# A two-layer vision tower on one core: order of small steps in three of its stages

## The chip, the cores and the metric

One Trainium2 chip, one of its cores. The metric is the device time of the program in microseconds (us), the median of several runs. The program is written out engine by engine: TensorE (PE), VectorE (DVE), ScalarE (ACT), GpSimd (POOL) and SyncE (SP) each have a queue of their own that runs in the order in which it is written, and the queues meet at semaphores.

## The reference

Four images of 3 x 224 x 224 become 4 x 3136 tokens of width 192. In short:

```python
h = conv_patches(x)                      # 4 x 4 patches, 192 wide
h = proj(softmax(q k^T / sqrt(96)) v)
n = layernorm(h)
q, k = elu(n Wq) + 1, elu(n Wk) + 1      # 64 wide, q times 1/8
F = clip(cumsum(log(sigmoid(n Wf + bf))), -20, 20)
num = q . (exp(F) cumsum(exp(-F) k v^T)) ;  den = q . (exp(F) cumsum(exp(-F) k)) + 1e-6
h = h + layernorm(num / den, gamma, beta) Wo
n = layernorm(h)
p = softmax(gelu(n w1 + b1) w2 + b2)     # 8 experts, the best two, renormalised
h = h + layernorm(n + sum_e p_e up_e(gelu(down_e(n))), gamma, beta)
n = layernorm(h)
q, k, v = split(n Wqkv)                  # q, k divided by their L1 sums over the tokens
h = h + (q (k^T v) per head) Wproj + b
n = layernorm(h)
h = h + bitlinear(silu(gate) * up)       # weights to -1, 0, 1; activations to 8 bits
```

All of it is computed in float32 or in pairs of rounded parts (a high part and a low part that is the rest), except for the rounded products of the last layer.

## The kernel before, in words

Tokens are handled in groups of 448 (four rows of 112 tokens), 7 to an image and 28 in all (`NC`). `h` stays in on-chip memory for all tokens. There are four stages, each with its own block of engine programs.

**Patch attention**, up to about 860 us. The change doesn't touch it.

**Routing stage** (`attend_route_phase`), a loop of 28 steps and a tail of three to four. In step g VectorE works on several groups at once: the decayed attention of group g and g+1, the addition of group g-1 into `h` (`add_out`, two halves), and the choice of experts for group g-3 (`largest`, `choose`, `take_rank`, `places`, `share`). `places` makes the row numbers at which a token's two copies go (`idx`), `share` (lines 1249 to 1254) the tickets: for each copy its gate and the number of its token. The queue of GpSimd has, in each step,

```python
if here(g - 4): scatter(g - 4, 0)   # waits for the ticket; copy, four indirect DMAs
if here(g - 1): factor(g - 1)       # waits for agg; veps, then rst (lines 712, 714)
if here(g):     add_bias(g)
if here(g - 4): scatter(g - 4, 1)
if here(g - 1): factor_route(g - 1)
```

`scatter` (lines 733, 737) copies the ticket behind the normalised rows and writes 448 rows to `rows_in` in DRAM. `factor` makes the scale `rst` of group g-1 from the aggregates `agg` (line 1147) that VectorE has made at the end of step g-1; `add_out` (line 1192) needs it. The first half of `add_out` releases the products into its PSUM bank on TensorE, whose chain (lines 842 to 847) ends in `den` (line 1127).

**Tile stage** (`tile_phase`): 63 tiles of 448 routed rows, each through one expert. SP loads the rows (`xb`) and the expert's weights (`wd`) two tiles ahead, TensorE transposes and multiplies, ScalarE makes high parts and gelu, VectorE the low parts (`take_low`, lines 1589 and 1590, and `lower`, line 1614), the copies of gate and home row (`take_tail`, lines 1599 to 1606) and half of the scaled result `yb` (`take_y`, line 1624). GpSimd gives the rows back to `rows_out` with four indirect DMAs a tile (line 1578). `take_tail(t+1)` waits until the give-back of tile t-3 has returned, since it overwrites the row numbers; `take_y(t-1)` waits for the same, since it overwrites `yb`. The load of tile t+2 waits for the tail of tile t.

**Last stage** (`attention_and_ffn_phase`), 28 steps and then the FFN. In a step, GpSimd starts two transfers that add the two expert rows of each token to what is in `sums` (`add_rows`), then one that adds beta to `h` (`add_bet`), all for five steps ahead; normalised rows are transposed, and `q_and_k` makes three products of which VectorE and ScalarE take L1 sums (`a_sum`, `b_sum`). Each image ends with its solution, five small links on TensorE (`turn_gram`, `keys_map`, `values_map`, `project_map`, `image_map`) that write to `pqk[1]`, the bank that also holds product m == 1 of `q_and_k`, so that each waits for `b_sum` in places. The Gram matrices have two banks `pg`. At the start GpSimd fills six constants, among them a row of ones of `xTB` (1 x 4480); VectorE sums and rounds the FFN's weights (`sum_weights`, from line 2425, and `round_weights`, up to line 2444) ahead of the loop.

Of the kernel before, what the change touches and what calls it, by code (L numbers as in the profile page):

```python
# [555 lines left out]
def attend_route_phase(nc, ins, h, bns, mean, rstd, minus, eye, held, tile_e, tile_r, down,  # L556
# [6 lines left out]
    with ExitStack() as ctx:  # L563
# [532 lines left out]
        def _(dve):  # L1096
# [218 lines left out]
            for g in range(NC + 3):  # L1315
# [19 lines left out]
                if here(g - 3):  # L1335
                    places(g - 3)
                    share(g - 3)
# [16 lines left out]
                if here(g):  # L1354
                    sums_stats(g, (2, 3))
                    sums_aggr(g)

# [18 lines left out]
def tile_phase(nc, ins, eye, down, tile_e, tile_r, rows_in, rows_out, held, returned):  # L1376

    with ExitStack() as ctx:
# [206 lines left out]
        def _(dve):  # L1585
# [65 lines left out]
def attention_and_ffn_phase(nc, ins, h, bns, mean, rstd, var, minus, eye, rows_out, out):  # L1651
# [9 lines left out]
    with ExitStack() as ctx:  # L1661
# [49 lines left out]
        pg = [ps(f"pg4_{i}", [128, 512]) for i in range(2)]  # L1711
# [45 lines left out]
        def pga(g, q):  # L1757
            return pqk[q % 2 if g else 0]

        pup = pg  # L1760
# [16 lines left out]
        NW = 5  # L1777
# [28 lines left out]
        def _(pool):  # L1806
            for n, (buf, value) in enumerate(((eps5[:], 1e-5), (mhalf[:], -0.5), (xTB[RB:RB + 1], 1.0),
                                              (wl[64:128, 1, :].bitcast(F32), 0.0))):
                nc.gpsimd.memset(buf, value).then_inc(S["w_ready"], 1)
                pool.wait_ge(S["w_ready"], n + 1)  # L1810
            nc.gpsimd.memset(ones[:], 1.0).then_inc(F["set"], 1)
            pool.wait_ge(F["set"], 1)
            nc.gpsimd.memset(mhalf5[:], -0.5).then_inc(F["set"], 1)
            pool.wait_ge(F["set"], 2)
# [34 lines left out]
            pool.wait_ge(S["e_in"], 32)  # L1849
            for s in range(-LEAD, NC):  # L1850
                if here(s + 5):
                    add_rows(s + 5, 0)
                if here(s + 3):
                    factor(s + 3)
                if here(s + 5):
                    add_bet(s + 5)
                    add_rows(s + 5, 1)
                if here(s + 2):
                    factor4(s + 2)

# [29 lines left out]
        def _(pe):  # L1890
            pe.wait_ge(S["w_in"], 16 * NW)
            pe.wait_ge(S["w_ready"], 4)
# [13 lines left out]
            def gram(g, b, c):  # L1906
# [3 lines left out]
                for q in range(TPC):  # L1910
                    for i in range(2):

                        mm = pe.matmul(pg[i][:, 0:(D, RB)[i]], xn[g % 2][:, q, i * 128:(i + 1) * 128],
# [841 lines left out]
```

## Time and profile before

| | |
|---|---|
| median of three runs | 2668.47 us (2668.48, 2668.47, 2664.71) |
| the profiled execution | 2666.92 us |
| its span, first to last instruction | 2665.1 us |
| mean granted clock of TensorE | 0.912 of full speed |
| busy: TensorE, VectorE, ScalarE, GpSimd | 2250.9, 1924.3, 1594.4, 1040.1 us |
| scatter transfers to `rows_in` (L737) | 224 instructions, 235.1 us on GpSimd |
| give-back transfers to `rows_out` (L1578) | 252 instructions, 244.5 us on GpSimd |

The profile has one row for a run of like instructions: start in us from the span's start, duration, engine, line, operation, names, and in brackets how long the engine was idle before it and what ended that idle time. A line number is one of the kernel before. Of an idle time the last releaser is named, and a name is that of the buffer that it wrote. A window row gives the busy time of each engine in a stretch, so engines that are all below the stretch's length are in a loop of waits.

### The profile page before, as it was taken

How to read it: one execution, taken by the hardware profiler on the slowest of the kernel's cores; microseconds unless marked ns; L12 is line 12 of the kernel's file. 1: busy time of each engine (PE TensorE's matmuls, PEld its weight loads, DVE VectorE, ACT ScalarE, POOL GpSimd, SP SyncE). 2: the span in 40 equal slices, each digit the busy share in tenths (PEclk: the TensorE clock that was granted, in tenths of full speed). 3: DMA queues.
4: the chain of work that ended last, by engine and by line, in shares of the span. 5: the costliest groups of instructions: out<-in, count | busy, mean ns of one | idle time of the engine just before them, and what ended most of it. 6: DMA issues, size and time to landing. Idle time of an engine off the chain costs nothing. (4 is left out here: it accounts for less than half of the span.)

```text
span 2665.1 us, 45416 instructions
## 1 busy us (share of the span) xinstructions
PE 2250.9 (84%) x14046; PEld 1626.4 (61%) x14047; DVE 1924.3 (72%) x5417; ACT 1594.4 (60%) x2815; POOL 1040.1 (39%) x1101
## 2 busy tenths in 40 slices
PE   8999999999997899999982999991778887766655
PEld 4444444444443788888871999991667775544443
DVE  5777777777774688888872566664558778889896
ACT  2444444444443688888861676663778764667776
POOL 1100100100000167667673577676555533353433
PEclk9999999999998899999985999996779998777777
DMA  2000000000000333233235677777756720000000
GB/s 59 0 19 13 0 18 13 1 9 1 0 0 23 87 66 75 67 73 76 66 71 165 219 242 240 246 242 133 94 71 87 91 30 6 22 22 26 22 27 26
DMA packets 114522, 183.08 MB, mean 69 GB/s; under 512 B 14337, under 2 KB 84326, under 8 KB 114078
## 3 DMA queue, kind: packets, MB, share of 16 engines
q0 software_dynamic: 74816, 86.34, 17.3%
q1 hardware_dynamic: 39554, 94.84, 11.1%
q8 instruction: 80, 1.31, 0.2%
q14 instruction: 72, 0.59, 0.1%
HBM read 64.44 MB, written 64.39 MB: 48 GB/s over the span
## 5 line engine op out<-in xcount | busy, mean ns | idle before, releaser
L213 ACT ACTIVATE prob<-pscore 128x896 f32<-128x896 f32 x336 | 308.1, 917 | 423.5 <-PE pscore L295 423.5
L420 DVE TENSOR_REDUCE pmax<-ppre 112x1 f32<-112x512 f32 x656 | 424.3, 686 | 162.0 <-PE ppre L262 161.9
L309 PE MATMUL pout<-prob,xkey 128*64 128x448 f32 x1344 | 328.0, 567 | 0.4 <-ACT prob L213 0.4
L1578 POOL DMA_INDIRECT rows_out<-yb,home3b x252 | 244.5, 970 | 141.8 <-issue 59.3
L262 PE MATMUL ppre<-xh,yh 49*112 49x512 f32 x656 | 291.3, 446 | 7.8 <-DVE pmax L420 4.1
L195 POOL CAST yh<-ynext 113x448 fp32r<-113x448 f32 x28 | 17.2, 616 | 667.3 <-DVE pmax L420 639.2
L737 POOL DMA_INDIRECT rows_in<-xr,idx x224 | 235.1, 1050 | 76.3 <-issue 44.8
L262 PEld LDWEIGHTS ppre<-xh,yh 49*112 49x112 f32 x656 | 112.6, 172 | 239.5 <-issue 103.5
L295 PE MATMUL pscore<-yh,xh 49*128 49x448 f32 x700 | 241.2, 422 | 0.4 <-DVE yh L440 0.4
L1872 POOL TENSOR_TENSOR sums<-rows,gout 112x512 f32<-112x512 f32 x112 | 141.2, 1270 | 253.2 <-DVE rows L2501 253.2
L295 PE MATMUL pscore<-yh,xl 49*128 49x448 f32 x700 | 202.9, 364 | 0.0
L295 PE MATMUL pscore<-yl,xh 49*128 49x448 f32 x700 | 142.8, 364 | 0.0
L2060 PE MATMUL ptr<-eyeb,wT 112*128 112x112 bf16 x448 | 45.3, 292 | 114.1 <-ACT wT L2253 114.1
L1485 PE MATMUL pz<-xth3b,wd 128*128 128x448 f32 x504 | 140.7, 381 | 0.0
L1500 PE MATMUL py<-uph,zl 128*112 x504 | 131.8, 261 | 0.0
L1500 PE MATMUL py<-upl,zh 128*112 x504 | 131.6, 261 | 0.0
L1500 PE MATMUL py<-uph,zh 128*112 x504 | 131.5, 261 | 0.0
L309 PEld LDWEIGHTS pout<-prob,xkey 128*64 128x64 f32 x1344 | 66.6, 135 | 105.7 <-issue 85.3
L295 PEld LDWEIGHTS pscore<-yh,xl 49*128 49x128 f32 x700 | 127.9, 187 | 0.8
L1935 PE MATMUL pqk<-xh,wh 128*128 128x448 f32 x168 | 72.1, 429 | 56.4 <-ACT spent L2196 55.8
L2060 PEld LDWEIGHTS ptr<-eyeb,wT 112*128 112x128 bf16 x448 | 38.9, 141 | 126.8 <-ACT wT L2253 88.9
L1472 PE MATMUL ptr3b<-eye,xb 112*128 112x112 f32 x504 | 63.5, 271 | 61.9 <-DMA xb<-rows_in 42.8
(393 smaller groups left out, 6647.2 us busy)
## 6 DMA issues: line engine op xcount, KB each, us to landing
wd<-down SPq DMA_DIRECT2D x63, 512.0 KB
xb<-rows_in SPq DMA_DIRECT2D x63, 455.0 KB
sums<-rows_out POOLq DMA_DIRECT2D x56, 336.0 KB, 6.1
h<-brow POOLq DMA_DIRECT2D x28, 336.0 KB, 5.2
h<-gambet POOLq DMA_DIRECT2D x28, 336.0 KB, 4.9
out<-sums SPq DMA_DIRECT2D x28, 336.0 KB, 2.8
rows_in<-zero SPq DMA_DIRECT2D x15, 455.0 KB, 5.5
rows_out<-yb,home3b POOLq DMA_INDIRECT x252
```

Of the source, the lines that this page charges most:

```text
L213: nc.scalar.activation(prob[j % 3][:, :, :], pscore[j % 2][:, :, 0:CH], ACT.Exp).then_inc(exped, 1)
L262: pe.matmul(out[:, :], yh1[rows, q * T:(q + 1) * T], xh[b % 2][rows, block * 512:(block + 1) * 512], start=True, stop=True, tile_position= ...
L295: mm = pe.matmul(pscore[j % 2][:, i, 0:CH], x[b % 2][rows, keys], y[rows], start=(n == 0), stop=(n == 2), tile_position=(i * LO, 0))
L309: mm = pe.matmul(pout[i * LO:(i + 1) * LO, 0:CH], xkey[b % 2][:, 2 * j + i, :], prob[j % 3][:, i, :], start=(j == 0), stop=(i == 1 and j = ...
L420: nc.vector.reduce_max(pmax[:, q, 2 * block + half:2 * block + half + 1], bank(u, depth), AX.X).then_inc(pre_max, 1)
L737: nc.gpsimd.indirect_dma_start(rows_in, bass.IndirectOffsetOnAxis(ap=idx[r % G3][:, 2 * q + k:2 * q + k + 1], axis=0), xr[r % G3][:, q, :] ...
L1485: mm = pe.matmul(pz[m][:, 0:CH], wd[i][:, w, cols], x, start=(s_ == 0), stop=(s_ == 4))
L1500: mm = pe.matmul(py[i][:, q // 2, (q % 2) * D:(q % 2 + 1) * D], zz[i][m][:, cols], w[:, bass.ds(2 * e + m, 1), :], start=(m + n == 0), sto ...
L1578: nc.gpsimd.indirect_dma_start(rows_out, bass.IndirectOffsetOnAxis(ap=home[r][:, q:q + 1], axis=0), yb[r % 2][:, q, :], None).then_inc(ret ...
L1872: nc.gpsimd.tensor_tensor(yg5[:, q, :], y[:, q, :], gout[:], ALU.mult).then_inc(F["yg_out"], 1)
L1935: mm = pe.matmul(pqk[m % 2][:, 0:CH], w, x, start=(n == 0), stop=(n == 4))
L2060: mm = pe.transpose(pyt[:, half, k * CH + q * T:k * CH + (q + 1) * T], yq[:, q, (2 * half + k) * 128:(2 * half + k + 1) * 128], eyeb[0:T, ...
```

## The change

Five things change. (1) In the routing stage VectorE's `share` goes, in the 28 full steps, from behind `places` to the very end of the step, behind the aggregates; `largest` waits for the earlier ticket to be done. GpSimd's queue there stays. (2) In the tile stage VectorE makes both sets of low parts first, then the copies of gate and home row. (3) In the last stage the two Gram banks become one and the solution gets a bank of its own, `psol`; waits of TensorE that kept the shared bank go. (4) The second accumulating transfer of a group is started one step after the first. (5) At that stage's start the row of ones comes by transfer, the constants are filled later, and the weight sums and rounding move to the ends of steps -1 and 0.

```diff
             def largest(r):
 
                 dve.wait_ge(R["ex_out"], r + 1)
+                if r:
+                    dve.wait_ge(R["tail_out"], r)
...
                 if here(g - 3):
                     places(g - 3)
-                    share(g - 3)
+                    if g >= NC:
+                        share(g - 3)
...
                 if here(g):
                     sums_stats(g, (2, 3))
                     sums_aggr(g)
+                    if here(g - 3):
+                        share(g - 3)
...
             def tile(t, r, n, last=False, enter=True):
                 i = r % 2
                 if not last:
-                    take_tail(t + 1, (r + 1) % 4, n + i)
                     take_low(t + 1, 1 - i)
                 lower(t, r)
+                if not last:
+                    take_tail(t + 1, (r + 1) % 4, n + i)
...
-        pg = [ps(f"pg4_{i}", [128, 512]) for i in range(2)]
+        pgram = ps("pg4", [128, 512])
+        pg = [pgram[:, 0:D], pgram[:, D:D + RB]]
+        psol = ps("psol4", [128, 512])
...
-        def pga(g, q):
-            return pqk[q % 2 if g else 0]
-
-        pup = pg
+        pga = pqk
+
+        def pup(g, q):
+            return (pgram, psol)[q % 2 if g else 0]
...
             for dst, name in ((wT, "wT4"), (wq, "wq4"), (wpT, "wpT4"), (heads[:], "heads"),
-                              (wimg[RB:RB + 1, 1, :], "bproj4")):
+                              (wimg[RB:RB + 1, 1, :], "bproj4"), (xTB[RB:RB + 1], "unit")):
                 sp.dma_start(dst, ins[name]).then_inc(S["w_in"], 16)
+            sp.wait_ge(both_in[0], 16)
...
-            pool.wait_ge(S["e_in"], 32)
             for s in range(-LEAD, NC):
                 if here(s + 5):
                     add_rows(s + 5, 0)
+                if here(s + 4):
+                    add_rows(s + 4, 1)
                 if here(s + 3):
                     factor(s + 3)
+                if s == -LEAD:
+                    pool.wait_ge(S["e_in"], 32)
                 if here(s + 5):
                     add_bet(s + 5)
-                    add_rows(s + 5, 1)
                 if here(s + 2):
                     factor4(s + 2)
+                if s == 1 - LEAD:
+                    constants(filled[2:3])
+                if s == -1:
+                    nc.gpsimd.memset(ones[:], 1.0).then_inc(F["set"], 1)
...
                     elif m == 1 and g:
                         pe.wait_ge(S["b_sum"], g)
-                        if b and c <= 2:
-                            pe.wait_ge(S[("t2_out", "m1_out", "wi_out")[c]], b)
...
             def turn_gram(b):
 
                 pe.wait_ge(S["g_out"], b + 1)
-                pe.wait_ge(S["b_sum"], CPI * (b + 1))
-                pe.transpose(pqk[1][:, 0:128], gsb[:, 0, D - 128:D], eye[:]).then_inc(S["gt_mm"], 1)
+                if b:
+                    pe.wait_ge(S["wi_out"], b)
+                pe.transpose(psol[:, 0:128], gsb[:, 0, D - 128:D], eye[:]).then_inc(S["gt_mm"], 1)
...
                 pe.wait_ge(S["t2_out"], b + 1)
-                if b + 1 < B:
-                    pe.wait_ge(S["b_sum"], CPI * (b + 1) + 1)
...
                 pe.wait_ge(S["m1_out"], b + 1)
-                if b + 1 < B:
-                    pe.wait_ge(S["b_sum"], CPI * (b + 1) + 2)
...
                 if 1 <= g * TPC + q <= TPC:
-                    pe.wait_ge(F["sg_out"], g * TPC + q)
+                    pe.wait_ge(F["y_out"], g * TPC + q)
...
-            weights_summed()
             for s in range(NC):
...
                 q_and_k(s, b, c)
+                if s == 0:
+                    weights_summed()
...
-            sum_weights()
-            round_weights()
             dve.wait_ge(S["e_in"], 32)
             for s in range(-3, NC):
...
+                if s == -1:
+                    sum_weights()
+                if s == 0:
+                    round_weights()
```

The order of VectorE's instructions at two places, and of GpSimd's at one. First VectorE in the middle of a full step of the routing stage, before (`idx` the row numbers, `ticket` the tickets, `gate` the forget gates' input):

```order
L1269 CAST idx_0<-row 112x8
L1249 SCALAR_TENSOR_TENSOR both<-total,both 112x4
L1252 TENSOR_SCALAR ticket_0<-home 112x8
L1253 RECIPROCAL both<-both 112x4
L1254 TENSOR_TENSOR ticket_0<-top,both 112x8
L1153 TENSOR_SCALAR gate<-pff,bff 128x448
```

And VectorE after the change, at the end of the step and the start of the next:

```order
L1147 BN_AGGR agg<-bn 112x2 x4
L1251 SCALAR_TENSOR_TENSOR both<-total,both 112x4
L1254 TENSOR_SCALAR ticket_0<-home 112x8
L1255 RECIPROCAL both<-both 112x4
L1256 TENSOR_TENSOR ticket_0<-top,both 112x8
L1183 TENSOR_TENSOR at<-pat,mask 112x448
L1234 TENSOR_REDUCE total<-ex 112x4
L1236 MAX top<-ex 112x8 x4
L1238 TENSOR_TENSOR both<-top 112x4
L1192 SCALAR_TENSOR_TENSOR h<-pvo,rst,h 112x192 x2
```

The four instructions of `share` have moved behind the aggregates; the half-add at line 1192 is the next step's.

VectorE in a tile of the tile stage, before:

```order
L1599 TENSOR_SCALAR other3b<-xb_1 112x4
L1601 COPY gate3b<-xb_1 112x4
L1604 TENSOR_TENSOR home3b<-xb_1,other3b 112x4
L1589 TENSOR_TENSOR xtl3b<-ptr3b,xth3b 128x448
L1590 TENSOR_TENSOR xth3b<-ptr3b,xth3b 64x448
L1614 TENSOR_TENSOR zl<-z_0,zh 128x448
L1614 TENSOR_TENSOR zl<-z_1,zh 128x448
L1624 TENSOR_SCALAR yb_1<-py_1,gate3b 112x192 x2
```

and after:

```order
L1594 TENSOR_TENSOR xtl3b<-ptr3b,xth3b 128x448
L1595 TENSOR_TENSOR xth3b<-ptr3b,xth3b 64x448
L1619 TENSOR_TENSOR zl<-z_0,zh 128x448
L1619 TENSOR_TENSOR zl<-z_1,zh 128x448
L1604 TENSOR_SCALAR other3b<-xb_1 112x4
L1606 COPY gate3b<-xb_1 112x4
L1609 TENSOR_TENSOR home3b<-xb_1,other3b 112x4
L1629 TENSOR_SCALAR yb_1<-py_1,gate3b 112x192 x2
```

The three instructions of the tail stand now directly ahead of `yb`.

GpSimd at the start of the last stage, after the change, with its waits (the six fills stood in a row ahead of the first transfer before):

```order
L1820 MEMSET eps_3 112x4
L1820 MEMSET mhalf 112x4 [waits w_ready_4]
L1833 DMA sums<-rows_out 112x4x192 [waits xa_out_4,w_ready_4]
L1838 DMA h<-gambet 112x4x192 [waits e_in_4]
L1833 DMA sums<-rows_out 112x4x192 [waits xa_out_4]
L1833 DMA sums<-rows_out 112x4x192 [waits rstd_out_3]
L1838 DMA h<-gambet 112x4x192
L1820 MEMSET wl 64x384
```

Four of the fills are behind the first transfers or gone, and the second transfer of the first group comes behind the first of the next.

## Rows read from the trace of the kernel before

**Rows 1.** Windows: start:end, length, busy (x instructions) of PE, PEld, DVE, ACT, POOL; PEclk, DMA share, GB/s

```profile
1150.00:1390.00 240.00, 227.03 (x1576) 202.04 (x1574) 203.77 (x872) 191.77 (x349) 168.82 (x202) 0.98 0.33 72
1472.60:1799.20 326.60, 313.93 (x2481) 297.23 (x2479) 204.55 (x501) 227.54 (x414) 228.12 (x235) 1.00 0.75 241
1823.00:1870.00 47.00, 4.09 (x18) 4.03 (x19) 23.56 (x71) 19.71 (x42) 31.88 (x32) 0.50 0.97 161
```

**Rows 2.** Timeline, VectorE, one step of the routing stage

```profile
1258.04 0.74 DVE L1192 SCALAR_TENSOR_TENSOR h<-pvo,rst,h 112x192 f32<-112x192 f32 x2 [0.24 <-POOL rst L714]
...
1264.81 0.23 DVE L1127 TENSOR_SCALAR den<-pvo 112x2 f32<-112x2 f32 x2 [0.39 <-PE pvo L847]
...
1267.26 0.15 DVE L1249 SCALAR_TENSOR_TENSOR both<-total,both 112x4 f32<-112x4 f32 x1
...
1267.82 0.68 DVE L1153 TENSOR_SCALAR gate<-pff,bff 128x448 f32<-128x448 f32 x1
...
1274.25 0.38 DVE L1147 BATCH_NORM_AGGREGATE agg<-bn 112x2 f32<-112x6 f32 x4
...
1276.14 0.74 DVE L1192 SCALAR_TENSOR_TENSOR h<-pvo,rst,h 112x192 f32<-112x192 f32 x2 [0.25 <-POOL rst L714]
```

**Rows 3.** Timeline, GpSimd, the same step

```profile
1275.06 1.05 POOL L714 TENSOR_TENSOR rst<-veps,mhalf 112x4 f32<-112x4 f32 x1
```

**Rows 4.** Timeline, TensorE, the same step

```profile
1257.96 1.47 PE L865 MATMUL pvo<-wo,nT 96*112 96x192 f32 x8
...
1264.28 0.49 PE L847 MATMUL pvo<-snap,qt 128*112 128x193 f32 x2
```

**Rows 5.** Timeline, VectorE, step 28 of the routing stage

```profile
1375.65 0.17 DVE L1254 TENSOR_TENSOR ticket<-top,both 112x8 f32<-112x8 f32 x1
...
1377.23 0.38 DVE L1147 BATCH_NORM_AGGREGATE agg<-bn 112x2 f32<-112x6 f32 x4
...
1382.76 0.74 DVE L1192 SCALAR_TENSOR_TENSOR h<-pvo,rst,h 112x192 f32<-112x192 f32 x2 [4.60 <-POOL rst L714]
```

**Rows 6.** Timeline, TensorE, two places of the last stage

```profile
1904.39 2.32 PE L1913 MATMUL pg<-xn 112*128 112x192 f32 x16
...
1925.97 0.74 PE L1935 MATMUL pqk<-xh,wh 128*128 128x448 f32 x1 [4.16 <-ACT spent L2196]
...
1929.49 3.34 PE L1913 MATMUL pg<-xn 112*128 112x192 f32 x16
```

**Rows 7.** Windows around those places

```profile
1926.00:1929.40 3.40, 3.40 (x13) 3.08 (x14) 0.79 (x2) 2.30 (x6) 2.27 (x2) 0.50 1.14 146
1932.90:1934.90 2.00, 2.00 (x10) 1.51 (x9) 1.50 (x7) 2.00 (x6) 0.93 (x2) 1.00 0.00 0
```

**Rows 8.** Waits, 1472.6 to 1799.2 us: total us, times, longest

```profile
DVE other3b L1599 <- DMA rows_out<-yb,home3b: 59.5, 29, 3.2
```

**Rows 9.** Timeline, VectorE, two tiles of the tile stage

```profile
1598.88 0.17 DVE L1599 TENSOR_SCALAR other3b<-xb 112x4 f32<-112x4 f32 x1 [2.07 <-DMA rows_out<-yb,home3b]
...
1600.48 1.38 DVE L1614 TENSOR_TENSOR zl<-z,zh 128x448 fp32r<-128x448 f32 x2
...
1609.93 0.23 DVE L1599 TENSOR_SCALAR other3b<-xb 112x4 f32<-112x4 f32 x1 [2.25 <-DMA rows_out<-yb,home3b]
```

**Rows 10.** Timeline, GpSimd, the first give-back between them

```profile
1602.91 0.93 POOL L1578 DMA_INDIRECT rows_out<-yb,home3b  x1 [1.00 <-DVE yb L1624]
```

**Rows 11.** Waits, TensorE, 1950 to 2200 us

```profile
PE pqk L1991 <- DVE sums L2583: 2.1, 3, 0.8
PE pqk L2009 <- DVE sums L2583: 1.8, 2, 0.9
```

**Rows 12.** Timeline, VectorE, start of the last stage

```profile
1834.20 0.06 DVE L2425 MEMSET wsum<- 128x4 f32 x1 [2.02 <-DMA xTA<-in_wout]
...
1844.07 0.56 DVE L2444 TENSOR_SCALAR woutq<-xTA 128x768 bf16<-128x768 f32 x1
```

**Rows 13.** Timeline, GpSimd, start of the last stage

```profile
1823.40 3.83 POOL L1809 MEMSET xTB<- 1x4480 f32 x1
```

More of the change, by code:

```diff
@@ L1776, in attention_and_ffn_phase @@
         block = ctx.enter_context(nc.Block())
-        NW = 5
+        NW = 6
         LEAD = 5
@@ L1806, in _, with constants @@
         def _(pool):
[L1807 to L1814, printed above, removed]
+            def constants(which):
+                for n, (buf, value) in which:
+                    nc.gpsimd.memset(buf, value).then_inc(S["w_ready"], 1)
+                    pool.wait_ge(S["w_ready"], n + 1)
+            filled = list(enumerate(((eps5[:], 1e-5), (mhalf[:], -0.5), (wl[64:128, 1, :].bitcast(F32), 0.0))))
+            constants(filled[0:2])
             def add_rows(g, k):
@@ L1852, in _ @@
                     add_rows(s + 5, 0)
+                if here(s + 4):
+                    add_rows(s + 4, 1)
                 if here(s + 3):
                     factor(s + 3)
+                if s == -LEAD:
+                    pool.wait_ge(S["e_in"], 32)
                 if here(s + 5):
                     add_bet(s + 5)
-                    add_rows(s + 5, 1)
                 if here(s + 2):
                     factor4(s + 2)
+                if s == 1 - LEAD:
+                    constants(filled[2:3])
+                if s == -1:
+                    nc.gpsimd.memset(ones[:], 1.0).then_inc(F["set"], 1)
+            nc.gpsimd.memset(mhalf5[:], -0.5).then_inc(F["set"], 1)
+            pool.wait_ge(F["set"], 2)
             def factor5(n, cols):
@@ L1891, in _ @@
             pe.wait_ge(S["w_in"], 16 * NW)
-            pe.wait_ge(S["w_ready"], 4)
+            pe.wait_ge(S["w_ready"], 3)
             def transposes(g):
@@ L1966, in turn_gram @@
                 pe.wait_ge(S["g_out"], b + 1)
-                pe.wait_ge(S["b_sum"], CPI * (b + 1))
-                pe.transpose(pqk[1][:, 0:128], gsb[:, 0, D - 128:D], eye[:]).then_inc(S["gt_mm"], 1)
+                if b:
+                    pe.wait_ge(S["wi_out"], b)
+                pe.transpose(psol[:, 0:128], gsb[:, 0, D - 128:D], eye[:]).then_inc(S["gt_mm"], 1)
             def two(i, cols):
-                return pqk[1][0:ROWS4[i], i * D:i * D + cols]
+                return psol[0:ROWS4[i], i * D:i * D + cols]
             def keys_map(b):
@@ L2013, in weights_summed @@
             def weights_summed():
-                pe.wait_ge(F["set"], 2)
+                pe.wait_ge(F["set"], 1)
                 pe.wait_ge(F["wc"], 1)
@@ L2042, in into @@
                 if 1 <= g * TPC + q <= TPC:
-                    pe.wait_ge(F["sg_out"], g * TPC + q)
+                    pe.wait_ge(F["y_out"], g * TPC + q)
                 if g == 1 and q == 1:
                     pe.wait_ge(S["wi_out"], B)
-                for dst, o, done in ((pga(g, q), HID, "in_mm"), (pup[q % 2], 0, "up_mm")):
+                for dst, o, done in ((pga[q % 2], HID, "in_mm"), (pup(g, q), 0, "up_mm")):
                     for c in range(2):
@@ L2069, in enter @@
                     pe.wait_ge(S["a_sum"], 2 * NC)
+                    pe.wait_ge(S["b_sum"], NC)
                     pe.wait_ge(S["g_out"], B)
@@ L2185, in copies @@
             def copies(g):
+                if g == 2:
+                    act.wait_ge(F["ready"], 3)
                 if g >= RING:
@@ L2218, in _ @@
                             act.wait_ge(S["t2_mm"], b)
-                        nc.scalar.copy(gsb[:, 0, :], pg[0][:, 0:D])
-                        nc.scalar.copy(gsb[0:RB, 1, 128:D], pg[1][0:RB, 0:RB]).then_inc(S["g_out"], 1)
+                        nc.scalar.copy(gsb[:, 0, :], pg[0])
+                        nc.scalar.copy(gsb[0:RB, 1, 128:D], pg[1][0:RB, :]).then_inc(S["g_out"], 1)
             def take_x(g):
@@ L2229, in silu @@
                     act.wait_ge(F["y_out"], g * TPC + q)
-                nc.scalar.activation(sg[q % 2 if g else 0], pga(g, q)[0:T], ACT.Silu, scale=dx[g % 2][:, q:q + 1]).then_inc(
+                nc.scalar.activation(sg[q % 2 if g else 0], pga[q % 2][0:T], ACT.Silu, scale=dx[g % 2][:, q:q + 1]).then_inc(
                     F["sg_out"], 1)
@@ L2355, in two @@
             def two(i, cols):
-                return pqk[1][0:ROWS4[i], i * D:i * D + cols]
+                return psol[0:ROWS4[i], i * D:i * D + cols]
             links = [0]
@@ L2429, in sum_weights, with round_weights @@
                 nc.vector.tensor_copy(eyeb[:], eye[:]).then_inc(F["ready"], 1)
+            def round_weights():
                 dve.wait_ge(F["wsum_mm"], 1)
@@ L2433, in sum_weights @@
                                         ALU.max).then_inc(F["wsc_out"], 1)
-            def round_weights():
                 dve.wait_ge(F["wsc_out"], 1)
@@ L2500, in gated @@
                 dve.wait_ge(F["sg_out"], g * TPC + q + 1)
-                nc.vector.scalar_tensor_tensor(y[:, q, :], pup[q % 2][0:T], dx[g % 2][:, q:q + 1], sg[q % 2 if g else 0],
+                nc.vector.scalar_tensor_tensor(y[:, q, :], pup(g, q)[0:T], dx[g % 2][:, q:q + 1], sg[q % 2 if g else 0],
                                                ALU.mult, ALU.mult).then_inc(F["y_out"], 1)
@@ L2739 @@
     lay["bproj4"] = f["L1_attn_b_proj"][None]
+    lay["unit"] = np.ones((1, CPI + 3, CH), np.float32)
     lay["win5"] = pieces(f["L1_ffn_w_in"].T)
```

4 lines of the change are left out of this document (2 added, 2 removed).

## The prediction

> **What bounds the kernel now.** I read the busy shares by stretch first. In the routing stage's 240 us [rows 1] TensorE is busy 227.0 us, VectorE 203.8, ScalarE 191.8 and GpSimd 168.8, at a clock of 0.98: no engine is full, so a step's length is that of a loop through several of them. In the tile stage [rows 1] TensorE is busy 313.9 of 326.6 us at full clock: TensorE bounds it, with 12.7 us of idle. At the start of the last stage [rows 1] TensorE works 4.1 of 47 us and the DMA engines 0.97 of the time: transfers bound it.
>
> Then the timeline of one step of routing. From one first half of the add into `h` to the next, 1258.04 to 1276.14, pass 18.10 us [rows 2]; that is the period. In it lie three stretches: the half-add to the denominators of the sums, 6.77 us (1264.81); the denominators to the end of the aggregates, 9.82 us (1274.25 + 0.38 = 1274.63); the aggregates to the next half-add, 1.51 us, which is GpSimd's `rst` [rows 3] (1275.06 + 1.05 = 1276.11) and nothing else. The half-add waits for it already: 0.24 and 0.25 us [rows 2]. So the chain aggregates, `rst`, half-add, TensorE's sums, aggregates closes on itself, and GpSimd's factor has no slack.
>
> **Tickets at the end of the step.** On GpSimd's queue each step begins with the first scatter of a group: it waits for the ticket, copies it, issues four indirect transfers, and only then comes `factor`, whose result the half-add needs. Before, `share` runs just ahead of the gate input at 1267.82 [rows 2], 6.8 us before the aggregates end, and the copy and the four transfers run beside VectorE's other work. Now `share` stands behind the aggregates that release `factor`. What is queued behind the late ticket is thus `factor` itself, and VectorE, then TensorE, wait for that.
>
> The trace holds this order once. At step 28 the stage's last steps leave VectorE little, and the ticket ends at 1375.65 + 0.17 = 1375.82; the half-add starts at 1382.76, after 4.60 us of waiting for `rst` [rows 5]. Ticket end to half-add is 6.94 us. The new period:
> - half-add to denominators, 6.77 less what TensorE was itself late with. The products that make its input end at 1257.96 + 1.47 = 1259.43 [rows 4], the half-add's pair at 1258.78 [rows 2]; with TensorE waiting instead, up to 0.44 goes: 6.33 (6.33 to 6.77).
> - denominators to aggregates, 9.82, loses `share`, 0.56 between 1267.26 and 1267.82 [rows 2]. But the gate and elu inputs that come next need products of TensorE that are barely done, so most of it turns into a wait; between all and nothing I give 0.2: 9.62 (9.26 to 9.82).
> - `share` itself at the end, four small instructions: 0.6.
> - ticket end to half-add: 6.94.
>
> Sum 23.49, so +5.4 us a step (5.0 to 6.1). It holds for groups 0 to 23, whose half-adds lie in steps 4 to 27: 24 x 5.4 = 130. In step 28 the ticket moves from 1375.82 to behind the aggregates, which end at 1377.61 [rows 5]: 1.8 later, once. Sum +132.
>
> **TensorE's clock.** These steps give TensorE an idle stretch that the stage does not have now (0.98 [rows 1]): between its products for the half-add and the first sum that needs it, about 5.4 us each step. What follows such a stretch is in the last stage's rows: TensorE waits 4.16 us and starts again at 1925.97 [rows 6]; in 1926.00 to 1929.40 its clock is 0.50, that is 1.2 GHz, and in 1932.90 to 1934.90 it is 1.00, 2.4 GHz [rows 7]. Sixteen matmuls of one shape take 3.34 us from 1929.49, against 2.32 at 1904.39 [rows 6]. Half speed thus lasted 3.4 to 5.1 us or more, worth 1.7 to 2.55 us of work at full speed. In routing that work is on the path: from the half-add on TensorE has few holes, the last product ending at 1264.77 [rows 4] for the denominators' start at 1264.81. I take 2.4 us a step, near the upper of the two, since TensorE's work there is dense; the ends are 0 (the clock holds) and 3.4 (all of the stretch and some of the next is slow). 24 x 2.4 = 58. With it the stage takes 132 + 58 = +190 (122 to 230).
>
> The Trainium skill, page "TensorE: Matmul & The Clock Gate", section "HAM oscillation — how this bites in real kernels", says that a loop of bursts parted by waits can start every burst slow again. By it the 58 us come in every step; if it failed here, only the 132 would be left. The rows of the last stage agree with it; none of routing shows it.
>
> **Tile stage.** Two tiles make a loop: take the tail of tile t+1 (waits for the give-back of t-3), lower its rows, lower its activations, scale t-1, give back. From 1598.88 to 1609.93 it takes 11.05 us [rows 9], 5.5 a tile. GpSimd's first give-back starts at 1602.91 [rows 10] and VectorE hears of its end at 1609.93, 7.0 us; the other 4.0 are VectorE's work and a hand-over. In every other tile it waits 59.5 us in 29 times for the return [rows 8]. Now the lowering of the rows and that of the activations (1.38 us at 1600.48 [rows 9], the other about as long) stand ahead of the wait. That leaves in the loop 4.0 - 2.6 = 1.4 and the 7.0: 8.4 for two tiles. At 5.53 a tile the stretch holds 59 tiles, and TensorE with 313.9 / 59 = 5.32 a tile is then the bound; GpSimd, whose transfer starts four times a tile and lasts 0.93 [rows 10] with a pause after it, is near it. So at most 12.7 us come back. I take -12 (-8 to -13). On SP's queue the load of the rows of tile t+2 waits for the tail of tile t, with the load of that tile's weights behind it. Both are issued after two lowerings more than now, though the wait ahead of them shrinks by about as much; where they land too late TensorE gives a part of the gain back, which is the end at -8.
>
> **The solution's own bank.** TensorE no longer waits for the sums ahead of two of the solution's links: 2.1 + 1.8 us over the three images whose solution lies between steps [rows 11]. The slower clock behind such waits is spared in part, so I take -6 (-4 to -9). The hand-over to the FFN waits a product of VectorE later for tiles 1 to 4 only: nothing, since the silu of the tile before already waits for the same product.
>
> **Start of the last stage.** The 3.83 us memset [rows 13] goes ahead of nothing any more and is a transfer now; the DMA engines being full [rows 1], an earlier issue is worth little. Weight sums and rounding ran from 1834.20 to 1844.07 + 0.56, 10.4 us [rows 12], beside transfers that were being waited for; now they stand between the first groups' work. The second accumulating transfer a step behind the first lets the first group through sooner. These have the same size and opposite signs: 0 (-6 to +5).
>
> **Sum** against the profiled execution, 2666.9 us, which lies 1.6 below the median of the runs: 2666.9 + 132 + 58 - 12 - 6 + 0 = 2838.9, rounded down to 2838.
>
> **The rivals.**
> - *The clock holds.* The wait is there but TensorE keeps 2.4 GHz: 2838 - 58 = 2780. For it: in routing the idle stretch is cut by small products. Against: the rows of 4.16 us [rows 6, 7]. Chance 0.18.
> - *Slow for longer.* 3.4 us a step and the sum's upper bounds, 9.5 x 24 = 228: 2666.9 + 230 - 12 - 6 = 2879 and up to 2895. Chance 0.08.
> - *The wait is absorbed, and it is faster.* GpSimd's transfers for the late ticket would have to end before `rst` is needed: the place is the half-add, the price 0, and it decides from where the half-add has 6.3 us of slack. Then tile stage and solution alone count: with the start's -5, 2666.9 - 12 - 6 - 5 = 2644. Against: half-adds that wait 0.24 us now, and 4.60 at step 28 [rows 2, 5]. Chance 0.04.
> - *Only part of it.* The largest selection or another engine moves and half the added wait hides: 2666.9 + 66 - 18 = 2715. Chance 0.02.
>
> **How the numbers follow.** The forecast, 2838, has 0.68. Its bounds are +122 to +230 for routing and -28 to -8 for the rest, 2761 to 2889. The range 2768 to 2888 takes in the forecast and the rival at 2780, and leaves out the absorbed wait, the half case and the end of the slow one. Runs of this kernel can tell 0.2 per cent, 5.3 us, from no change. Faster by more is the absorbed wait, 0.04; within it 0.01, where the half case is smaller still; slower 0.95.
>
> **What would show it.** The half-add of each step waits 4 to 6 us for `rst`, and `rst` starts behind four scatter transfers that start behind the ticket; the period is 24 to 27 us; the stage's clock falls from 0.98 to under 0.95 with half speed behind each half-add; in the tile stage TensorE is busy over 0.99 and VectorE's 59.5 us of waits for returned rows fall below 20; the solution's waits for the sums are gone. I am wrong if the period stays near 18.1, if the half-add finds `rst` ready, or if the tile stage is not shorter while routing is as forecast.

## The result and the profile after

The changed kernel takes 2830.27 us (median of four: 2828.01 to 2836.00) against 2667.72 (median of four) for the kernel before. The ratio is 1.0615, with a 95% interval of 1.0596 to 1.0633. The forecast was 2838, and the range of 2768 to 2888 holds the time. The profiled execution took 2836.0 us with a span of 2834.2, so it lies 5.7 above its median.

From here on a line number is one of the kernel of the run that is read; the same instruction can have another number in another run.

Where the time went shows already in the rows of GpSimd's give-back, since the first and the last of these transfers mark the tile stage. In the trace of the kernel before, all instructions of its line (starts of the first and of the last behind the durations):

```profile
L1578 POOL DMA_INDIRECT rows_out<-yb,home3b x252: 924/932/1366, 1474.5 to 1820.2; - x126
```

The same of the changed kernel:

```profile
L1583 POOL DMA_INDIRECT rows_out<-yb,home3b x252: 925/932/1343, 1664.0 to 1989.0; - x126
```

Up to the first give-back 189.5 us are added. The tile stage shrinks from 345.7 to 325.0 us, by 20.7. What is left of the span behind it is 844.9 before and 845.2 after. 189.5 - 20.7 + 0.3 = 169.1, the difference of the spans.

Windows of the changed kernel: start:end, length, busy (x instructions) of PE, PEld, DVE, ACT, POOL, clock, DMA share, GB/s. The first answers to the first of [rows 1], the second is 59 tiles and answers to its second; the others follow each other through two steps of routing.

```profile
1150.00:1390.00 240.00, 188.16 (x1185) 168.03 (x1185) 151.76 (x624) 143.90 (x269) 106.45 (x136) 0.87 0.23 49
1662.00:1966.00 304.00, 303.88 (x2473) 294.35 (x2472) 204.38 (x499) 226.94 (x413) 229.71 (x234) 1.00 0.82 257
...
1161.00:1165.10 4.10, 0.00 (x0) 0.00 (x0) 0.00 (x0) 0.04 (x1) 3.39 (x5) 1.00 0.36 111
1165.10:1171.90 6.80, 5.58 (x21) 5.40 (x22) 3.89 (x22) 1.94 (x5) 5.60 (x7) 0.50 0.60 106
1171.90:1189.00 17.10, 14.85 (x105) 12.87 (x104) 12.06 (x44) 13.10 (x23) 4.35 (x7) 1.00 0.07 21
1189.00:1195.80 6.80, 3.31 (x10) 3.23 (x11) 3.89 (x22) 1.10 (x4) 5.71 (x8) 0.50 0.51 83
1195.80:1216.30 20.50, 16.01 (x115) 14.01 (x114) 12.04 (x44) 13.96 (x25) 7.96 (x11) 1.00 0.16 46
```

In routing every engine is busy less than before in the same 240 us, TensorE by 17% (188.2 us against 227.0) and GpSimd by 37% (106.5 against 168.8), and the clock is 0.87 instead of 0.98. Nothing has become the bound but the loop of waits.

VectorE in a step of routing, the rows that answer to [rows 2]:

```profile
1165.52 0.74 DVE L1192 SCALAR_TENSOR_TENSOR h<-pvo,rst,h 112x192 f32<-112x192 f32 x2 [5.81 <-POOL rst L714]
...
1174.66 0.23 DVE L1127 TENSOR_SCALAR den<-pvo 112x2 f32<-112x2 f32 x2 [0.39 <-PE pvo L847]
...
1183.85 0.38 DVE L1147 BATCH_NORM_AGGREGATE agg<-bn 112x2 f32<-112x6 f32 x4
...
1184.59 0.17 DVE L1256 TENSOR_TENSOR ticket<-top,both 112x8 f32<-112x8 f32 x1
...
1191.70 0.74 DVE L1192 SCALAR_TENSOR_TENSOR h<-pvo,rst,h 112x192 f32<-112x192 f32 x2 [5.83 <-POOL rst L714]
...
1199.73 0.23 DVE L1127 TENSOR_SCALAR den<-pvo 112x2 f32<-112x2 f32 x2 [0.39 <-PE pvo L847]
```

GpSimd between the ticket and that half-add:

```profile
1184.83 0.19 POOL L733 COPY xr<-ticket 112x8 f32<-112x8 f32 x1 [11.47 <-DVE ticket L1256]
1185.59 1.01 POOL L737 DMA_INDIRECT rows_in<-xr,idx  x1 [0.57 <-POOL xr L733]
...
1189.37 0.93 POOL L737 DMA_INDIRECT rows_in<-xr,idx  x1 [0.30 <-issue]
1190.32 0.21 POOL L712 TENSOR_TENSOR veps<-agg,eps 112x4 f32<-112x4 f32 x1
1190.62 1.05 POOL L714 TENSOR_TENSOR rst<-veps,mhalf 112x4 f32<-112x4 f32 x1
```

And TensorE around the same wait:

```profile
1185.65 1.47 PE L865 MATMUL pvo<-wo,nT 96*112 96x192 f32 x8
1192.49 1.01 PE L842 MATMUL pst<-vt,ktok 112*128 112x193 f32 x2 [5.38 <-DVE h L1192]
1193.30 0.85 PE L844 MATMUL pvo<-vt,at 112*112 112x193 f32 x2
...
1198.20 0.49 PE L847 MATMUL pvo<-snap,qt 128*112 128x193 f32 x2
```

GpSimd stands idle for 11.47 us until the ticket comes. Then the copy and four transfers go out, and only behind them `rst`, though the aggregates were done at 1184.23. VectorE waits 5.83 us for it, TensorE 5.38 us for VectorE. TensorE then works at half clock (0.50, 1.2 GHz) until 1195.8: two small matmuls take 0.85 there, 0.49 at 1198.20.

Waits of VectorE in the 59 tiles, 1662 to 1966 us (total, times, longest), against [rows 8]:

```profile
DVE xtl3b L1594 <- ACT xth3b L1533: 67.5, 59, 1.3
...
DVE other3b L1604 <- DMA rows_out<-yb,home3b: 1.2, 3, 0.6
```

The prediction counted 59.5 us of VectorE's waits for returned rows [rows 8]. In the other tiles the trace of before has another 49.0 us, ahead of the copy of the gate:

```profile
DVE gate3b L1601 <- DMA rows_out<-yb,home3b: 49.0, 29, 3.3
```

So 108.5 us of waiting for returned rows have become 1.2. VectorE now waits for ScalarE's high part instead, which costs nothing here, since TensorE is busy 303.9 of 304.0 us.

Waits of TensorE in the last stage, 2119 to 2369 us, against [rows 11]; the waits for the sums ahead of the links are gone:

```profile
PE pqk L1951 <- ACT spent L2213: 34.5, 19, 4.1
PE psol L1985 <- ACT maps L2237: 1.1, 2, 0.5
```

### The profile page after: what moved, and what is told of

It reads as the page before. It is cut to its first block and busy times, and to the rows that moved or that the text cites. A ratio compares the mean times of both kernels' runs of the same rounds, so it can differ in the third digit from the quotient of the medians.

```text
span 2834.2 us, 45431 instructions
## 1 busy us (share of the span) xinstructions
PE 2313.0 (82%) x14046; PEld 1683.6 (59%) x14047; DVE 1923.2 (68%) x5417; ACT 1594.0 (56%) x2815; POOL 1016.4 (36%) x1100
## 5 line engine op out<-in xcount | busy, mean ns | idle before, releaser
L737 POOL DMA_INDIRECT rows_in<-xr,idx x224 | 213.4, 953 | 76.3 <-issue 45.1
L842 PE MATMUL pst<-vt,ktok 112*128 112x193 f32 x224 | 82.3, 460 | 131.5 <-DVE h L1192 130.5
L1037 ACT COPY snap<-pst 128x193 f32<-128x193 f32 x112 | 36.0, 321 | 211.0 <-PE pst L842 210.2
L1192 DVE SCALAR_TENSOR_TENSOR h<-pvo,rst,h 112x192 f32<-112x192 f32 x112 | 41.5, 413 | 149.1 <-POOL rst L714 148.6
L842 PEld LDWEIGHTS pst<-vt,ktok 112*128 112x128 f32 x224 | 48.5, 255 | 143.3 <-DVE h L1192 138.2
```

Of the source, the lines that this page charges most:

```text
L737: nc.gpsimd.indirect_dma_start(rows_in, bass.IndirectOffsetOnAxis(ap=idx[r % G3][:, 2 * q + k:2 * q + k + 1], axis=0), xr[r % G3][:, q, :] ...
L842: pe.matmul(pst[:, 0:V1], ktok[:, q, :], vt[:, q, :], start=(reset and q == 0), stop=True, skip_group_check=True).then_inc(S["st_mm"], 1)
```

## The experiments

**One: the tickets back.** The changed kernel with the first part undone.

```diff
-                    if g >= NC:
-                        share(g - 3)
+                    share(g - 3)
...
                     sums_aggr(g)
-                    if here(g - 3):
-                        share(g - 3)
...
                 dve.wait_ge(R["ex_out"], r + 1)
-                if r:
-                    dve.wait_ge(R["tail_out"], r)
```

> The changed kernel with the tickets (share) back in the middle of the step; tile stage and last stage as changed. Ticket theory: the routing stage's +189 us are all from the ticket's place. The step is 18.1 us again, and the time is that of the kernel before less the tile stage's 21 us, 2643 to 2650. Rival (a part of the loss comes from elsewhere, such as a slower start of the tile stage or the last stage): 2670 or more.

Measured: 2640.7 us, 0.9911 of the kernel before (0.9890 to 0.9932). That is 189.6 below the changed kernel, the same as the 189.5 of the two traces' first give-backs, and 2 us below my window. By the two ratios to the kernel before, measured side by side with each, it is 188 us. The whole loss comes with the ticket's move, and without it the change is a gain. The move has two parts, the ticket's place and the new wait in `largest`; the second experiment keeps both and tells them from the queue.

**Two: the same late ticket, another queue on GpSimd.**

```diff
+                if here(g - 1):
+                    factor(g - 1)
                 if here(g - 4):
                     scatter(g - 4, 0)
-                if here(g - 1):
-                    factor(g - 1)
                 if here(g):
                     add_bias(g)
+                if here(g - 1):
+                    factor_route(g - 1)
                 if here(g - 4):
                     scatter(g - 4, 1)
-                if here(g - 1):
-                    factor_route(g - 1)
```

> The changed kernel, tickets as late as in it, but GpSimd's queue in each step is factor, first scatter, bias, factor_route, second scatter. Theory A, the cost is what stands behind the ticket on GpSimd's queue: the half-add waits under 1 us, the step is 18.0 to 18.6 us and the time 2640 to 2662. Rival B, the lateness of the ticket itself costs (the scatters and what waits for them come too late, or VectorE's order is the limit): the step stays at 23 us or more and the time at 2770 to 2835. Rival C, the scatters only swap places and now hold up factor_route, which the offset needs: a step of 20 to 22 us, 2690 to 2740.

Measured: 2649.4 us (2642.5 to 2661.3), 0.9942 of before (0.9924 to 0.9960). VectorE at one step's end:

```profile
1222.17 0.38 DVE L1147 BATCH_NORM_AGGREGATE agg<-bn 112x2 f32<-112x6 f32 x4
...
1222.91 0.17 DVE L1256 TENSOR_TENSOR ticket<-top,both 112x8 f32<-112x8 f32 x1
...
1224.14 0.74 DVE L1192 SCALAR_TENSOR_TENSOR h<-pvo,rst,h 112x192 f32<-112x192 f32 x2
```

GpSimd in the same step:

```profile
1222.98 1.04 POOL L714 TENSOR_TENSOR rst<-veps,mhalf 112x4 f32<-112x4 f32 x1
1224.00 0.18 POOL L733 COPY xr<-ticket 112x8 f32<-112x8 f32 x1
...
1230.83 1.04 POOL L723 TENSOR_TENSOR rstd<-veps3r,mhalf 112x4 f32<-112x4 f32 x1
```

The last instruction of the ticket still starts 0.74 us behind the aggregates' last, and `largest` still waits for it; `rst` is done at 1224.02, and the half-add follows without a wait. The steps alternate between 17.8 and 18.7 us, 18.24 in the mean. So a late ticket costs the step next to nothing by itself; what it cost was that `factor` stood behind the scatter, which waits for the ticket. Rivals B and C fall. The edit moves both scatters, and the runs do not tell their shares apart. In the two traces the first give-back comes at 1478.4 us here and at 1472.9 in the first experiment: 5.5 us, of which 24 steps of 0.14 us are 3.4. The medians differ by 8.7 us, but the two intervals overlap, and the first experiment's own kernel, run once more (ten), came out 8.7 us higher too; I read no more into it.

**Three and five: TensorE kept busy in the gap.** The clock's share of the loss can be taken out alone: the wait stays, but TensorE does small products that nobody reads. Their place and number:

```diff
                 if 0 in tiles:
+                    if 4 <= g < NC:
+                        for _ in range(44):
+                            pe.matmul(pqk[:, CH:CH + 64], eye[:], eye[:, 0:64], start=True, stop=True,
+                                      skip_group_check=True)
                     if g:
                         pe.wait_ge(S["h_half"], g)
```

> The changed kernel with 44 small products on TensorE (64 columns, into columns of a bank that nobody reads) ahead of its wait for the half-add in steps 4 to 27, so that TensorE is not idle there. Added work: the result does not use it. Clock theory: the wait stays at some 5.8 us, but the stretch from half-add to denominators falls from 9.1 to 6.4-7.0 us, the stage's clock rises from 0.87 to over 0.95, and 24 steps give back 50 to 65 us: 2765 to 2780. Rival, the stretch is longer for another reason (order, memory traffic) and the clock reading only goes with it: 2825 to 2840, or longer if the small products run past the wait.

Measured: 2877.1 us, a miss. The sizing was wrong. Its row on TensorE in one step:

```profile
1200.44 9.94 PE L833 MATMUL pqk<-eye 128*128 128x64 f32 x88
```

I had counted one matmul each at about 0.1 us; the trace has two for each, 113 ns apart. They run to 1210.38, 4.5 us past the end of the half-add (1205.18 + 0.74), and the step is 27.6 us. The median says nothing on the question, since the added work hides what the clock gives. Two rows of the run do speak to it:

```profile
1210.22 0.55 PE L846 MATMUL pst<-vt,ktok 112*128 112x193 f32 x2
```

```profile
1215.82 0.23 DVE L1131 TENSOR_SCALAR den<-pvo 112x2 f32<-112x2 f32 x2 [0.39 <-PE pvo L851]
```

From TensorE's first sum to the denominators pass 5.60 us, where the changed kernel needs 7.24 (1192.49 to 1199.73) and 8.34 (1166.32 to 1174.66). To see it in the time, the run was made again with `range(22)`.

> As e3_warm, with 22 small products instead of 44. In e3_warm they took 9.94 us a step (each is two matmuls of 113 ns) and ran 4.3 us past the half-add, which hid what the clock gave. 22 take 5.0 us, inside TensorE's 5.3 to 5.4 us of waiting. Clock theory: half-add to denominators 9.1 to under 6.8 us, a step of 23.4 to 23.9 us instead of 26, 2765 to 2785. Rival (the longer stretch has another reason): 2825 to 2840.

Measured: 2782.5 us (2770.3 to 2787.7), 47.8 below the changed kernel, or 47 by the ratios to the kernel before (1.0440 and 1.0615). VectorE in a step:

```profile
1193.07 0.74 DVE L1196 SCALAR_TENSOR_TENSOR h<-pvo,rst,h 112x192 f32<-112x192 f32 x2 [5.82 <-POOL rst L714]
...
1199.52 0.23 DVE L1131 TENSOR_SCALAR den<-pvo 112x2 f32<-112x2 f32 x2 [0.39 <-PE pvo L851]
...
1209.45 0.17 DVE L1260 TENSOR_TENSOR ticket<-top,both 112x8 f32<-112x8 f32 x1
...
1216.54 0.74 DVE L1196 SCALAR_TENSOR_TENSOR h<-pvo,rst,h 112x192 f32<-112x192 f32 x2 [5.82 <-POOL rst L714]
```

And its window in routing:

```profile
1150.00:1390.00 240.00, 230.91 (x1703) 210.54 (x1703) 163.45 (x678) 154.26 (x286) 121.63 (x155) 1.00 0.26 57
```

VectorE's wait is the same (5.82 us beside 5.81 to 5.83), the clock is 1.00, and half-add to denominators takes 6.45 us, where the changed kernel alternates between 8.0 and 9.1. The period is 23.5 us in all but four of the 24 steps. So the wait costs some 5.4 us a step and the slow clock behind it 2.2 more. In the two traces the first give-back comes 56.5 us earlier here (1607.5 against 1664.0), which is the clock's whole share of routing; the median shows less of it because the last stage of this trace took 5.7 us longer (850.9 against 845.2) with the same code.

**Four: the tile pass alone**, on the kernel before.

> The kernel before with the tile pass's new order alone. The stage's give-backs went from 345.7 to 325.0 us between the two traces. Theory: all of it is the order of VectorE's pass, 2645 to 2649 (-19 to -22 us). Rival 1, TensorE's busy time caps the gain at 12.7 us as I took it, and the rest came with another state of memory in that run: 2654 to 2658. Rival 2, the gain comes back as a later start of the last stage: 2664 or more.

Measured: 2645.5 us, 0.9914 of before (0.9896 to 0.9933). The window over 59 tiles:

```profile
1472.60:1776.60 304.00, 304.00 (x2476) 294.82 (x2475) 203.93 (x499) 226.76 (x413) 230.00 (x234) 1.00 0.81 258
```

The whole gain is there, and more than the 12.7 us that I took as its cap. One pair of traces overstates it somewhat: first to last give-back took 345.7 us in the trace of before, but 343.2 and 342.3 in those of experiments six and seven, whose tile stage is the same, and 323.9 to 325.1 in all nine traces with the new pass. The gain is thus 17 to 22 us.

**Eight: the tail between the two lowerings**, on the kernel before.

```diff
-                    take_tail(t + 1, (r + 1) % 4, n + i)
                     take_low(t + 1, 1 - i)
+                    take_tail(t + 1, (r + 1) % 4, n + i)
                 lower(t, r)
```

> The kernel before with the tail copies in the tile pass behind the lowering of the rows but ahead of that of the activations. Theory: once TensorE is the bound the rest of the order is free. The loop over two tiles is 7.0 + 1.4 + 1.4 = 9.8 us, under TensorE's 10.3 for two tiles (5.15 each in the changed kernel), so the gain is that of the full move, -19 to -22: 2644 to 2648. Rival: both lowerings have to be ahead of the wait, since the second holds up the activations' products; half of the gain, 2653 to 2658.

Measured: 2640.8 us, 0.9917 of before (0.9893 to 0.9942). Its window over the tiles:

```profile
1472.60:1776.60 304.00, 304.00 (x2476) 294.76 (x2474) 206.67 (x496) 226.57 (x413) 227.92 (x235) 1.00 0.79 258
```

And VectorE's waits for the returns in it:

```profile
DVE other3b L1599 <- DMA rows_out<-yb,home3b: 27.7, 29, 2.2
DVE gate3b L1601 <- DMA rows_out<-yb,home3b: 27.3, 29, 1.5
```

VectorE still waits 55 us for the returns, half of the 108.5 before, and it costs nothing: the stage takes 324.6 us against 324.4 in experiment four. By the sum that was written down for it the loop over two tiles is 9.8 us here, under TensorE's 10.3; with that, both orders tried are worth the same. The rival falls.

**Six: the solution's bank alone**, on the kernel before: all hunks of the diff on `psol`, `pgram`, `pga`, `pup` and the waits of TensorE on them, and no others.

> The kernel before with the solution's own bank and the waits that it spares alone. Theory (my term): -4 to -9 us, since TensorE's waits for the sums ahead of two links, 3.9 us, go: 2657 to 2663. Rival 1: the links are paced by the copies between them and by VectorE, and nothing comes back: 2665 to 2668. Rival 2: the FFN's first tiles wait for y instead of the silu and cost 1 to 3 us, 2667 to 2670.

Measured: 2657.6 us (twelve runs), 0.9977 of before (0.9960 to 0.9993), that is -2 to -11 us with -6.1 in the middle. The theory's figure is met; the first rival lies at the edge of the interval, the second outside. The traces show where the gain is. All Gram products of the stage, before and here (starts of the first and of the last behind the durations):

```profile
L1913 PE MATMUL pg<-xn x448: 218/326/634, 1868.4 to 2201.4; 112*128 112x192 f32 x75, 112*128 112x64 f32 x75
```

```profile
L1916 PE MATMUL pg<-xn x448: 218/326/634, 1863.8 to 2187.5; 112*128 112x192 f32 x75, 112*128 112x64 f32 x75
```

From the last give-back (1820.2 and 1816.3) to the last Gram product pass 381.2 us before and 371.2 here, 10 us less, though TensorE's waits for the sums were 3.9. What the other 6 are was not tried. What follows, the FFN above all, took 463.7 us before and 472.5 here and hides it in this trace; in the twelve traces it took from 461.7 to 474.6 us, with the new bank or without.

**Seven: the start of the last stage alone**, on the kernel before.

> The kernel before with the last stage's start alone: row of ones by transfer, constants later, second accumulating transfer a step later, weight sums and rounding at the ends of two steps. My term was 0. Between the two traces the first Gram product came 3.0 us earlier in its stage (45.2 after 48.2) and the third step's 5.6 later (77.3 after 71.7). Theory: these cancel, 2662 to 2670. Rival: the last-stage gain of e1_share_back over e4_tile_only, 4.8 us, is this part's: 2660 to 2663.

Measured: 2664.5 us, 1.0013 of before (0.9998 to 1.0029), which is -1 to +8 us: no gain, perhaps a small loss. What happens there can be read in the changed kernel's trace, VectorE:

```profile
1998.32 0.79 DVE L2423 CAST wh<-wT 128x384 fp32r<-128x384 f32 x3 [15.97 <-DMA xTB<-in_unit]
...
2020.48 1.14 DVE L2309 BATCH_NORM_STATS2 bn<-sums 112x6 f32<-112x192 f32 x4 [8.51 <-DMA sums<-rows_out]
...
2049.01 0.16 DVE L2451 TENSOR_SCALAR wsc<-po 128x1 f32<-128x1 f32 x1 [1.61 <-PE po L2031]
```

The weights' split waits for the last of the small loads, now the row of ones (15.97 us, up to 1998.32). VectorE still waits over 8 us for the summed rows, and the rounding (from 2049.01, 60 us into the stage) stands between the first groups. The first Gram product starts 3.0 us earlier in its stage than before, the third 5.6 later. In the trace of this run itself it is 4.5 earlier and 3.9 later, and the last one starts 378.9 us behind the last give-back, against 381.2 before.

**Nine and ten: the best of the parts.** Tile pass and bank without the start, beside the first experiment's kernel again.

> The kernel before with the tile pass's order and the solution's bank, without the new start and without the tickets' move. If the parts add, 2663 - 21 - 6 = 2636 to 2641, and 0 to 3 us under the version with the start. Rival: the last stage absorbs the tile stage's gain or the bank's, over 2645.

> The kernel of e1_share_back once more beside e9_tile_and_bank, which differs by the start of the last stage alone. If the start is worth nothing (e7_start_only), both agree within 3 us; if the start's cancelling parts lean to a gain beside the new bank, this one is 3 to 6 us faster.

Measured: 2637.7 us, 0.9876 of before (0.9850 to 0.9903), and 2649.4 us, 0.9921 (0.9893 to 0.9948). The parts add, as written down for nine. For ten neither of the two outcomes came: it was to agree within 3 us or to be 3 to 6 faster, and its median is 11.7 slower. The profiled executions of the two differ by 0.2 us in span (2636.6 and 2636.4), and the kernel of e10 had shown 2640.7 in e1. These runs scatter more than the earlier ones (the kernel before: 2656.8 to 2680.6).

The traces say a little more. From the last give-back to the last Gram product:

| last stage | us, by trace |
|---|---|
| as before (before, e4, e8) | 381.2, 381.5, 383.2 |
| start alone (e7) | 378.9 |
| bank alone (e6, e9) | 371.2, 368.5 |
| bank and start (changed kernel, e1, e2, e3, e10, e5) | 374.7, 376.1, 376.1, 374.7, 374.7, 383.0 |

Without the start the bank is worth 10 to 15 us in this stretch; with it, 5 to 9 in five of six traces. So the start costs some 4 to 8 us beside the new bank, and by itself it shows no cost there. In the whole time this stays suggested, not settled, since what follows varies by more. The start brings nothing in any run's time. The version with the tile pass and the bank alone has the lowest ratio here, 1.2% under the kernel before, but its interval overlaps that of the first experiment (0.9890 to 0.9932).

## Why the prediction was right

**The ticket.** Each term of the step can be set beside a row:

| | forecast, us | measured |
|---|---|---|
| half-add to denominators, full clock | 6.33 | 6.45 (e5) |
| denominators to end of aggregates | 9.62 | 9.57 (1174.66 to 1184.23) |
| end of aggregates to end of ticket | 0.6 | 0.53 (to 1184.76) |
| end of ticket to half-add | 6.94 | 6.94 (to 1191.70) |
| slow clock | 2.4 | 2.2 (e5 against the changed kernel) |
| period | 25.9 | 25.7, as 25.1 and 26.2 in turn |
| last step, 27 to 28 | +1.8 | +6.3 (22.47 against 16.14); +2.0 at full clock (e5) |
| stage | +190 | +189.5 |

The one place in the trace of before at which the new order already occurred, step 28 [rows 5], gave the price exactly, because GpSimd's chain from ticket to `rst` is the same instructions with nothing beside them. The pauses between the transfers, which a sum of durations leaves out, are in it.

That the stage came out at +190 to the half microsecond is in part luck. The 24 steps grew by 183.3 us, where 187 were forecast, and the step behind them by 6.3 instead of 1.8; the prediction had charged the slow clock to the 24 steps alone. Some small readings in it are off as well, without changing the forecast: the stretch of 1.51 us ahead of the half-add holds `veps` and two hand-overs besides `rst`; the upper end of a step is 6.0 us by its own terms, not 6.1, and the upper end of the rest -7, not -8; the rival's "up to 2895" lies above its own upper bound of 2889.

**The clock.** The rival in which the clock holds, 2780, is what e5 measures with the clock restored (2782.5); in the changed kernel it doesn't hold. The Trainium skill, page "TensorE: Matmul & The Clock Gate", section "HAM oscillation — how this bites in real kernels", says that a loop of bursts parted by waits can start every burst slow again; the trace agrees: each burst behind the wait started at 0.50 in the rows shown. I took 58 us; it was 48 by the medians and 56.5 by the first give-backs, of which 52.1 lie in the 24 steps and 4.3 in the one behind them. The length was read from the last stage as 3.4 to 5.1 us. The same rows give 5.6: 3.5 us from 1925.97 to 1929.49, and twice the 1.02 us by which the sixteen matmuls are longer than at full speed [rows 6]. The changed kernel has this length in every other step (1166.32 to 1171.9) and 3.3 us in the steps between (1192.49 to 1195.8). Half of their mean is the 2.2 us a step that e5 gave back.

**The absorbed wait** needed 6.3 us of slack at the half-add. There was none, and e2 shows what it takes to get it: not an earlier ticket but another order on the queue of the engine that waits for it.

**Tile stage, mis-sized.** The term that was mis-sized is "TensorE with 313.9 / 59 = 5.32 a tile is then the bound", and with it "at most 12.7 us come back". Measured: 20.7 us by the give-backs of the two traces (17 to 22 over all), 20.9 by the medians of e4, and 5.15 us a tile (304.0 / 59). The direction and the mechanism were right. The work of TensorE did not shrink. Groups of its instructions in the 59 tiles, before (count, busy us, mean ns, idle before):

```profile
L1485 PE MATMUL pz<-xth3b,wd 128*128 128x448 f32 x472 | 129.7, 376 | 0.0
...
L1472 PE MATMUL ptr3b<-eye,xb 112*128 112x112 f32 x472 | 57.3, 264 | 12.3 <-DVE xth3b L1590 11.8
```

and in the changed kernel:

```profile
L1490 PE MATMUL pz<-xth3b,wd 128*128 128x448 f32 x472 | 129.5, 376 | 0.0
...
L1477 PE MATMUL ptr3b<-eye,xb 112*128 112x112 f32 x472 | 55.1, 259 | 0.1
```

The instructions are the same in number and all but the same in length; the 12.3 us of idle are gone, and 10 us of busy time with them. Single matmuls of the stage overlap their neighbours. In the changed kernel the last product of a tile and the first transposition of the next pass follow at the pace of all others, 0.10 us from start to start, with 0.26 us each:

```profile
1801.72 0.26 PE L1505 MATMUL py<-upl,zh 128*112 x1
1801.82 0.93 PE L1477 MATMUL ptr3b<-eye,xb 112*128 112x112 f32 x8
```

Before, the two are further apart in 43 of the 58 tiles of which the trace has both, for example:

```profile
1599.81 0.25 PE L1500 MATMUL py<-upl,zh 128*112 x1
1600.50 0.32 PE L1472 MATMUL ptr3b<-eye,xb 112*128 112x112 f32 x1 [0.44 <-DVE xth3b L1590]
```

From start to start pass 0.69 us, 0.59 more than without the wait. Of that only 0.44 shows as idle; the other 0.15 is under the record of the matmul ahead and counts as busy. Summed over the stretch, these distances are 24.4 us before and 5.9 in the changed kernel, and those within the transpositions 42.0 and 39.8: together 20.7 of the 22.6 us by which the 59 tiles are shorter, and only 12.3 of it showed as idle. So TensorE's own work needs no more than 5.15 us a tile, and a pause between two starts that is shorter than a matmul's own tail leaves no gap in the busy time.

**The bank**, -6 forecast; measured -5.4 by the medians of e6, -6.1 by its ratio, with the interval from -2 to -11. **The start**, 0 forecast; measured +1.5 by the medians of e7, +3.5 by its ratio.

**The sum.** 190 - 12 - 6 + 0 forecast, 189.6 - 20.9 - 5.4 + 1.5 = 164.8 from the medians of the single experiments, 162.6 between those of the two kernels. The forecast was 7.7 us too high, nearly all of it the tile stage. In the profiled execution the bank's gain doesn't appear in the length of the last stage (845.2 us, against 840.1 and 839.5 with the same code in e1 and e10). It is there up to the last Gram product, 374.7 us against 381.2, and the FFN behind it is the longer by that much in this trace (470.5 against 463.7).

## What to carry to other kernels

When an instruction moves, look less at the engine that issues it than at the in-order queue that waits for it: list what stands behind that wait, and ask whether any of it feeds the loop that sets the period. A place in the old trace where the new order happens by accident is worth looking for: here it gave the price to the hundredth, pauses included. When a queue serves both a closed loop and a side output, put the loop's piece first; then the side output may be late, which here cost 18.2 us a step instead of 25.7.

Of an engine with overlapping instructions, the busy time of a stretch is an upper bound of what it needs, not the need itself. The starts of its instructions tell more: where one follows a wait, compare its distance to the one ahead with the usual distance.

## What was not expected of the hardware

The same wait of 5.4 us is followed by half speed of two lengths in turn. TensorE is idle from 1187.1 to 1192.49; the clock falls at 1189.0 and is 1.00 again from 1195.8. In the step before it is idle from 1161.0 to 1166.32; the clock is 1.00 until 1165.1, then 0.50 to 1171.9. So 3.3 us of half speed fall on work behind the one wait and 5.6 us behind the other. The stretch from half-add to denominators is 8.03 and 9.14 us accordingly, and the steps are 25.1 and 26.2 us in turn.

A float32 matmul of 64 columns is two matmuls in the trace of e3, 113 ns apart, so 44 of them took 9.94 us; that spoiled its median.
